# Moving the stores of groups 2 and 3, and their 24 stack loads, from SyncE to GpSimd in an attention layer

## The reference, cut to what matters

```python
q, k, v = (proj(W, b) for W, b in ((Wq, bq), (Wk, bk), (Wv, bv)))   # (B, heads, N, head_dim)
scale = 1.0 / jnp.sqrt(jnp.float32(HEAD_DIM))
scores = jnp.einsum('bhqd,bhkd->bhqk', q, k) * scale
attn = jax.nn.softmax(scores, axis=-1)
ctx = jnp.einsum('bhqk,bhkd->bhqd', attn, v)
out = jnp.einsum('bhwc,dc->bhwd', ctx, Wo) + bo
```

## Time and profile before

| | |
|---|---|
| median of 3 runs | 561.25 us (558.76 to 562.37) |
| span of the profiled execution, first to last instruction | 559.4 us |
| TensorE busy | 420.8 us (75%) |
| VectorE busy | 355.7 us (64%) |
| ScalarE busy | 289.4 us (52%) |
| GpSimd busy | 102.5 us (18%) |
| mean DMA rate | 61 GB/s |

### The profile page before, as it was taken

The page is one execution under the profiler, slowest core; times in us unless marked ns, Lnnn a source line. Parts: engine busy times, 40 slices in busy tenths (PEclk is TensorE's granted clock), DMA queues, the critical chain, the costliest instruction groups (busy, mean ns, idle before and its releaser), DMA issues. The chain is left out here.

```text
span 559.4 us, 9015 instructions
## 1 busy us (share of the span) xinstructions
PE 420.8 (75%) x3218; PEld 210.9 (38%) x3218; DVE 355.7 (64%) x670; ACT 289.4 (52%) x509; POOL 102.5 (18%) x106
## 2 busy tenths in 40 slices
PE   1426761599999638398879999964639999999995
PEld 1114551246455314233323333332314545455442
DVE  4447786332466587896649999433155878788784
ACT  1359964131432315136548788840646858487441
POOL 3510004000000003511112211110002707337000
PEclk9756995599999876858879999995957999999999
DMA  5300000800000001933510000007747091561402
GB/s 137 109 0 1 0 0 0 182 6 1 1 0 1 0 0 39 255 97 110 154 30 2 4 2 2 4 0 166 176 96 163 1 220 35 127 129 42 87 2 75
DMA packets 22649, 34.35 MB, mean 61 GB/s; under 512 B 5377, under 2 KB 17873, under 8 KB 21841
## 3 DMA queue, kind: packets, MB, share of 16 engines
q1 hardware_dynamic: 19920, 29.67, 21.9%
q10 hardware_dynamic: 2688, 4.16, 3.4%
HBM read 16.80 MB, written 4.64 MB: 38 GB/s over the span
## 5 line engine op out<-in xcount | busy, mean ns | idle before, releaser
L880 DVE TENSOR_REDUCE L_mx<-L_ring 128x2 f32<-128x512 f32 x128 | 83.5, 687 | 22.2 <-PE L_ring L1003 21.6
L1262 DVE TENSOR_TENSOR L_s<-L_row_ps,L_cols 128x1024 f32<-128x1024 f32 x72 | 87.7, 1219 | 8.3 <-PE L_row_ps L1393 6.7
L935 ACT ACTIVATE L_e<-L_ring 128x512 f32<-128x512 f32 x128 | 73.6, 598 | 32.1 <-PE L_ring L1016 30.1
L1414 PE MATMUL L_acc<-L_s,L_t_sb 128*64 128x256 f32 x576 | 79.8, 399 | 1.1 <-DVE L_s L1262 1.0
L1323 ACT ACTIVATE L_cols<-L_col_ps 128x512 f32<-128x512 f32 x72 | 42.8, 596 | 45.6 <-PE L_col_ps L1401 45.3
L1003 PE MATMUL L_ring<-stacks_k_st,stacks_q_st 64*128 64x256 bf16 x256 | 53.3, 311 | 7.4 <-DMA stacks_k_st<-L_k_parts 6.9
L1016 PE MATMUL L_ring<-stacks_q_st,stacks_k_st 64*128 64x256 bf16 x256 | 49.3, 293 | 7.6 <-DMA stacks_q_st<-L_m_parts 7.6
L1414 PEld LDWEIGHTS L_acc<-L_s,L_t_sb 128*64 128x64 f32 x576 | 35.5, 138 | 35.1 <-DVE L_s L1262 21.2
L1393 PE MATMUL L_row_ps<-L_hats,L_sel 48*128 48x512 bf16 x144 | 44.6, 392 | 0.0
L1036 PE MATMUL L_ctx_ps<-L_e,L_v_x 128*32 128x256 f32 x512 | 42.9, 410 | 0.0
L1384 PE MATMUL L_acc<-all_w_all,L_xn 64*128 64x192 f32 x96 | 26.3, 356 | 13.9 <-DVE L_t_sb L1242 13.9
(11 more groups left out here) (250 smaller groups left out, 737.4 us busy)
## 6 DMA issues: line engine op xcount, KB each, us to landing
L_hats<-L_parts SPq DMA_DIRECT2D x32, 216.0 KB, 5.0
L_hat<-L_offsets SPq DMA_DIRECT2D x24, 192.0 KB, 4.5
stacks_q_st<-L_q_parts SPq DMA_DIRECT2D x24, 128.0 KB, 3.1
L_mask<-L_offsets SPq DMA_DIRECT2D x12, 192.0 KB, 4.7
L_q_parts<-L_parts SPq DMA_DIRECT2D x8, 192.0 KB, 3.0
L_k_parts<-L_parts SPq DMA_DIRECT2D x8, 192.0 KB, 3.2
stacks_k_st<-L_k_parts ACTq DMA_DIRECT2D x12, 128.0 KB, 4.2
stacks_k_st<-L_k_parts SPq DMA_DIRECT2D x12, 128.0 KB, 2.9
```

What stands on the lines that cost most here:

```text
L880: dve.tensor_reduce(mx[:, n % 2, :, head], ring[:, place(step) % 3].rearrange("p (q s) -> p q s", q=2), AX.X, ALU.max).then_inc(max_read, 1)
L935: act.activation(e[:, k], ring[:, 3 + v % 3], ACT.Exp, scale=HD2 ** -0.5).then_inc(e_ready, 1)
L1262: dve.tensor_tensor(s[:, q], row_ps[:, q], cols[:, t % 3:t % 3 + 1].broadcast_to([P, 2, 2 * N]), ALU.mult).then_inc(s_ready, 1)
L1414: mm = pe.matmul(acc[C * e:C * e + C, b, 0:N], t_sb[:, b, h, (KK * e + t) * C:(KK * e + t + 1) * C], s[:, q, h, e * N:(e + 1) * N], start= ...
```

## The change

`store_parts` becomes a function of the issuing engine, and `load_stacks` gets a slice of slots. SyncE keeps the stores and q loads of groups 0 and 1; all maxima are now sent by its loop, which starts at group 0. GpSimd issues the stores of groups 2 and 3 (8 DMAs) behind its last L837, and behind its work on each of images 0 to 5 four loads: two of q and two of k, of group 2 for images 0 to 2, of group 3 for images 3 to 5. Line numbers move: stores L794 become L779, loads L782 become L789, L845/L847/L850 become L837/L839/L842, and L837 becomes L827.

```diff
-        def load_stacks(eng, g, s):
+        def store_parts(eng, g):
+            for s in range(2):
+                eng.wait_ge(parts_ready, 2 * g + s + 1)
+                for b in range(2):
+                    dst = scratch[s][g].rearrange("t e d p b n -> b (e d p) t n")[b]
+                    eng.dma_start(dst, parts[C * b:C * b + C, g, s]).then_inc(stored[2 * g + s], 16)
+
+        def load_stacks(eng, g, s, slots=(0, 6)):
             eng.wait_ge(stacks.filled, 2 * g + 2)
             eng.wait_ge(stored[2 * g + s], 32)
-            for slot, part in enumerate(((0, 0, 0, 1, 1, 2), (0, 1, 2, 0, 1, 0))[s]):
+            for slot, part in list(enumerate(((0, 0, 0, 1, 1, 2), (0, 1, 2, 0, 1, 0))[s]))[slots[0]:slots[1]]:
...
-                store_parts(0)
+                store_parts(sp, 0)
                 load_stacks(sp, 0, 0)
-                store_parts(1)
+                store_parts(sp, 1)
                 load_stacks(sp, 1, 0)
-                send_maxima(0, 0)
-                store_parts(2)
-                send_maxima(0, 1)
-                load_stacks(sp, 2, 0)
-                send_maxima(0, 2)
-                load_stacks(sp, 2, 1)
-                store_parts(3)
-                send_maxima(0, 3)
-                load_stacks(sp, 3, 0)
-                load_stacks(sp, 3, 1)
-                with sp.Fori(1, NQ) as i:
+                with sp.Fori(0, NQ) as i:
                     for j in range(4):
                         send_maxima(i, j)
...
                         pool.tensor_tensor(parts[:, g, s, 2], rest[:, g % 2, s], parts[:, g, s, 1], ALU.subtract).then_inc(parts_ready, 1)
+                store_parts(pool, 2)
+                store_parts(pool, 3)
                 pool.wait_ge(pool_own, 2)
...
+                    if n < 6:
+                        g, third = 2 + n // 3, n % 3
+                        load_stacks(pool, g, 0, (2 * third, 2 * third + 2))
+                        load_stacks(pool, g, 1, (2 * third, 2 * third + 2))
```

More of the change, by code:

```diff
@@ L787, in _ @@
                 sp.sem_inc(m_stacked, 128)
[L789 to L794, removed]
                 def send_maxima(i, j):
```

## The result

The changed kernel takes 545.0 us at the median (542.76 to 548.9, four runs), the kernel before 560.29 beside it; the ratio is 0.974 (95% interval 0.970 to 0.979). Later rounds gave the unchanged pair 0.981 (0.975 to 0.986) and 0.979 (0.974 to 0.985). Over all 14 runs of the changed kernel the median is 548.5 us, and they reach from 542.76 to 551.66. Ratios leave out executions more than 1.5% above the fastest of their kernel, which are two of the ten of e2_sp_idle_issues and one of the four of e7_straight; the traces of these two kernels are of such an execution.

What follows compares the result with a forecast made beforehand. SyncE's issue time, which delays the maxima TensorE waits for in layer 2, was taken as the bound. Freeing it (-13.3 us) plus GpSimd's hidden issues (0) gave 548.0 us from 561.25, range 546.0 to 556.5.

Steps and rivals of the forecast that it cites:

- the term for the scatter: Whole kernel: runs scatter by about 2 us to either side, which set the range's low end at 546.0 us.
- layer 3 as before: Sign in the later profile: layer 2 shorter by 13 us, layer 3 unchanged.
- The forecast's own term: Layer 2, images 3 to 6: SyncE without the moved stores and loads saves 13.3 us; forecast case's chance 0.45.
- GpSimd's price: Time one DMA issue takes on GpSimd: 1.1 us assumed, between 0.59 and 1.54; cost to the kernel 0.
- rival C: GpSimd's DMAs: dearer issues (1.3 to 1.7 us) or a first-issue cost lose part of the gain; 550 to 556; chance 0.20.
- The cover of the stores: GpSimd before image 0's maxima: eight stores take 8.8 us and fit into 9.6 us free; cost 0.
- the rings were not near their limit: DMA rings in layer 2: busy share 0.46 at most, so stores starting during group 1's loads cost 0.
- no wait over 0.3 us: Sign in the later profile: TensorE never waits over 0.3 us for the maxima.
- A (GpSimd the bound): GpSimd's stream in layer 2 becomes the limit, break-even at 1.8 us per issue, 568.4 us at 2.0; chance 0.07.
- lateness formula: GpSimd, six images: lateness is six times an image's GpSimd time beyond 6.92 us, plus late stores, less about 1 us slack.
- B (VectorE holds the issues up): GpSimd's issues in layer 2 each wait for a VectorE instruction, up to 1.28 us; time 549.6; chance 0.20.
- D: Whole kernel: same time, 561 us, the stalls being hidden behind another limit; chance 0.08.

Runs made afterwards that it cites:

- e2_sp_idle_issues: Changed kernel, with SyncE also issuing 32 DMAs of 1 KB to a spare tile where stores and loads had stood; 562.97 us, ratio 1.005 to the kernel before.
- e7_straight: Changed kernel with the maxima of images 0 to 3 written out on SyncE's queue instead of sent by the loop; 547.57 us, ratio 0.974.
- e1_again: The changed kernel once more, no edit, beside the kernel before; 549.09 us, ratio 0.981.
- e11_again: The changed kernel a third time, no edit, beside the kernel before; 548.03 us, ratio 0.979.
- e3: Changed kernel with only the 8 stores on GpSimd; SyncE keeps the 24 loads among the maxima; 555.21 us, ratio 0.993.
- e8: Changed kernel with GpSimd's stores behind images 0 and 3 and its loads one image later, images 1 to 6; 546.57 us, ratio 0.975.
- e6: Changed kernel with twelve more 1 KB DMAs on GpSimd for each of images 0 to 5, 16 issues an image; 565.07 us, ratio 1.006.

## Why the prediction was wrong, and where it was right

**The failed step is the term for the scatter, which set the low end of the range**: "runs scatter by about 2 us to either side", taken from the three runs shown. One program's executions differ by 8.9 us here (542.76 to 551.66), the kernel before's by 7.4 (556.11 to 563.54 in one set of 23). The sum put what lies outside layer 2 at nothing ("layer 3 as before"). In the profiled pair it was 5.0 us, of which 3.95 ahead of layer 2; e1_again and e11_again, with layer 2 starting at 211.94 and 207.47 us, show that such a gain does not belong to the change. The profile before could have warned in part: its clock is at half in slices ahead of layer 2, and the traces later differed where the clock fell. Four runs of the changed kernel happened to hold 542.76 and 542.94; the profiled one is the first of these, with layer 2 starting 3.1 and 7.5 us earlier than in the other two traces. A range of 4 us to either side of 548.0 would have held all three medians (545.0, 549.09, 548.03).

The base, 561.25, was a median of three of such runs as well; the median beside the changed kernel was 560.29, which is 1.0 us of the miss, and later medians of the kernel before are 556.64 to 560.56. So that the median of all 14 runs, 548.5, lies so near to 548.0 is in part luck: the base was above every later median of the kernel before. By the three ratios the change is worth 14.3, 10.7 and 11.5 us, each to within about 3 us; 13.3 was forecast.

**The forecast's own term was right.** Predicted from the trace before: -13.28 us for images 3 to 6. Measured in the traces: 34.04 to 20.47, -13.57, and 20.47 to 20.49 in all three traces of the changed kernel. Stalls, refill and clock went together, as the 6.92 us of an undisturbed image said. That SyncE's issue time makes them is shown by e2 and e3. For the whole of layer 2 the three traces give 13.4, 13.3 and 11.3 us.

**GpSimd's price was over-estimated without harm.** Taken 1.1 us, bounds 0.59 to 1.54; measured 0.48 to 0.51 for a load and 0.63 for a store, so for loads even below my lower end. A first-issue cost of rival C shows as 0.2 us (836 ns against 630; the same in e1_again). The Trainium skill's figure of about 1 us to the first byte ("DMA: Bandwidth & Descriptors", "Latency and other measured facts") is a latency. It does not bound what the issue takes of GpSimd's time, and from issue to landing GpSimd's loads (q and k) took 2.7 and 3.0 us at the median, SyncE's 3.1 and 2.9 before. No run here shows the time to the first byte.

**The cover of the stores was costed too well.** I wrote that the rings were not near their limit, 0.46 at most by the earlier trace rows. Those windows begin at 258 us; the page has a 9 for the DMA in the 17th slice, 224 to 238 us, where group 1's loads run and where the stores now start. In the first walk of the changed kernel the share reaches 0.93. Two things were late by it. ScalarE's last loads held back its copy of image 0's maxima, which started 2.05 us behind the start of the turn instead of 0.68. And the maxima reached TensorE 2.16 us behind their last issue instead of 1.08. (The other two traces have 1.5 and 2.0 us for the copy, 1.8 and 1.6 for the maxima.) TensorE waited 1.73 us, so my sign "no wait over 0.3 us" failed at image 0. e3 and e8 tell the two apart. e3 keeps the early stores and has the late copy (2.05 us), but no loads behind image 0: its maxima take 1.08 us and TensorE waits 0.23. e8 has the copy in time (0.68 us), but stores behind image 0: 2.0 us and a wait of 1.24. So most of the new wait comes from what GpSimd issues in the same moment as SyncE's small transfers, which my sum had put at nothing, and not from a first-issue cost, as which I would have read it.

The stretch from layer 2's start to image 3 takes 50.6 to 52.5 us in three traces, against 50.1 and 50.5 before and 49.6 in e3: a cost of 0.2 to 2.4 us where I had put 0. How much of it is the clock is open. In the first trace the clock was full from 248 us on, where I had 254; four of these six us are the earlier start of the layer.

**The rivals.** A (GpSimd the bound): shown as a mechanism in e6, not reached by the change. Its lateness formula at 9.0 us an image gives 6 x (9.0 - 6.92) = 12.5 us; layer 2 was 15.3 longer. B (VectorE holds the issues up): no sign; GpSimd's loads take 481 to 541 ns beside VectorE's L877. This agrees with the rule that excludes reductions (the Trainium skill, "SBUF — State Buffer", "Who interferes with whom"); whether another instruction of VectorE would hold an issue up is not shown by any run here. C: no issue took 1.3 us, and the first cost 0.2 us more; its price was not seen. D: not seen.

**Left open.** Why the clock holds through a 1.47 us gap in one execution and not in the next was not settled; nor which part of the remaining scatter comes from layer 1's start.

## What to carry to other kernels

Look at what stands in a queue in front of a small, urgent DMA: 12 issues of 0.6 us held back four of 2 KB, and idle issues did so as well as real ones. Here an engine with idle time took such issues over at 0.5 to 0.6 us each. Its own work plus issues must stay below the time of an image: with eight issues (about 5.3 us of work in 6.9) no cost could be told from scatter, with sixteen (9.0 us) the gain was gone. Check as well what the engine now issues in the moment in which the next urgent transfer goes out: four loads beside image 0's maxima made these arrive 0.5 to 1.1 us later. And take a kernel's scatter from many runs before drawing a range: three runs showed 3.6 us of a spread of over 7.

## What the runs showed of the hardware

- A DMA issued by GpSimd takes it 481 to 541 ns (128 KB load, 16 rows) and 630 to 638 ns at the median (192 KB store); the first one 833 to 836 ns (the changed kernel's three traces). The profile lists them in GpSimd's own row, not in a queue's, and counts them as busy time.
- Behind a copy that had waited for TensorE, GpSimd's next load started 0.21 us later (four of four in the changed kernel's trace); behind one that had not, at once. A store behind such a copy started at once (e8, 266.26 us).
- The same gap of 1.47 us on TensorE was followed by matmuls at 1.99 us in one execution and 3.78 us in another of the same program.
- Stores issued by GpSimd while another group's loads run took 6.8 and 7.4 us to land (median of four each), where SyncE's took 3.0 and 3.2 before; issued by GpSimd with less beside them (e8, image 0) they took 3.2 and 3.4.
- Four DMAs of 2 KB reached TensorE 1.08 us behind their last issue in the kernel before and in e3, and 1.6 to 2.2 us (three traces of the changed kernel) with four loads of 128 KB issued beside them by GpSimd.
